# A graph layer on one core: the first four quads of the round gathered from the input rows during setup, and the weights loaded as six arrays

## The reference

```
h  = relu(layernorm(x))                       # 6250 x 128: 32 scalars, 32 vectors of 3
s  = h[:, :32] @ W_up_s / sqrt(32);  v = (h[:, 32:] as u x 3) through W_up_v / sqrt(32)
tpw = silu(silu(ef @ A1 + b1) @ A2 + b2) @ A3 # per edge, 4 x 32 weights w0..w3
message of an edge: s[src], v[src] times edge_attr and w0..w3   # 256 values
agg = segment_sum(message, dst) / 10
out = x + (agg through W_out_s, W_out_v) / sqrt(64)
```

## Time and profile before

| | us |
|---|---|
| median of 3 runs | 1932.57 (1929.12 to 1933.47) |
| the profiled execution, its own time | 1928.3 |
| its span | 1926.5 |

### The profile page before, as it was taken

The page is one execution under the profiler, slowest core; times in us unless marked ns, Lnnn a source line. Parts: engine busy times, 40 slices in busy tenths (PEclk is TensorE's granted clock), DMA queues, the critical chain, the costliest instruction groups (busy, mean ns, idle before and its releaser), DMA issues. The chain is left out here.

```text
span 1926.5 us, 69847 instructions
## 1 busy us (share of the span) xinstructions
PE 1632.5 (85%) x22862; PEld 1289.1 (67%) x22862; DVE 1340.1 (70%) x2623; ACT 403.3 (21%) x640; POOL 1424.7 (74%) x1558
## 2 busy tenths in 40 slices
PE   5898879888898898798988987988889879888895
PEld 3677667667676676676766766767667657666673
DVE  5767767676677676776776866767768667676684
ACT  4222212221122121221211211212212212222221
POOL 4777777777777777777777777777777777777774
PEclk9898889898898898998988988989889889898897
DMA  8222222222222222222222222222222222222223
GB/s 244 63 67 63 69 68 62 65 70 61 66 64 69 67 64 63 71 60 68 63 68 67 63 65 70 61 66 67 66 67 63 66 69 62 65 68 63 67 63 107
DMA packets 127196, 136.87 MB, mean 71 GB/s; under 512 B 74779, under 2 KB 96852, under 8 KB 126678
## 3 DMA queue, kind: packets, MB, share of 16 engines
q0 software_dynamic: 48096, 97.92, 20.2%
q1 hardware_dynamic: 78134, 33.75, 7.0%
q10 hardware_dynamic: 576, 0.05, 0.0%
HBM read 125.14 MB, written 6.43 MB: 68 GB/s over the span
## 5 line engine op out<-in xcount | busy, mean ns | idle before, releaser
L626 POOL DMA_INDIRECT rows<-node_table,src_in x1491 | 1407.7, 944 | 464.4 <-issue 457.3
L909 PE MATMUL pss<-tab_sb,x_sb 128*128 128x128 f32 x4704 | 635.1, 292 | 0.0
L909 PEld LDWEIGHTS pss<-tab_sb,x_sb 128*128 128x128 f32 x4704 | 598.5, 206 | 13.4 <-issue 0.2
L876 PEld LDWEIGHTS psw<-a_bd,h 64*128 64x128 f32 x3136 | 230.2, 201 | 355.6 <-DVE msgs L775 171.7
L876 PE MATMUL psw<-a_bd,h 64*128 64x128 f32 x3136 | 316.0, 318 | 146.8 <-DVE msgs L775 136.0
L773 DVE TENSOR_TENSOR msgs<-rows,psw 128x256 f32<-128x256 f32 x392 | 165.2, 421 | 363.5 <-PE psw L876 182.1
L775 DVE TENSOR_TENSOR msgs<-rows,psw 128x768 f32<-128x768 f32 x392 | 371.3, 947 | 0.0
L748 DVE TENSOR_TENSOR x_sb<-picks_in,psx 128x1024 f32<-128x1024 int32 (+1 forms) x294 | 363.1, 1236 | 0.0
L897 PE MATMUL pss<-msgs,onehot 128*32 128x64 f32 (+1 forms) x12544 | 325.0, 249 | 0.0
L669 ACT ACTIVATE sums<-pss 128x384 f32<-128x384 f32 (+1 forms) x196 | 90.7, 463 | 1037.2 <-PE pss L909 805.7
L897 PEld LDWEIGHTS pss<-msgs,onehot 128*32 128x32 f32 x12544 | 256.0, 117 | 53.6 <-issue 10.1
(11 more groups left out here) (67 smaller groups left out, 312.8 us busy)
## 6 DMA issues: line engine op xcount, KB each, us to landing
rows<-node_table SPq DMA_DIRECT2D x3072, 0.5 KB
rows<-node_table,src_in POOLq DMA_INDIRECT x1491
ef_in<-in_efT SPq DMA_DIRECT2D x100, 96.0 KB
picks_in<-in_picks SPq DMA_DIRECT2D x50, 64.0 KB
attr_in<-in_attr SPq DMA_DIRECT2D x100, 32.0 KB
xT_sb<-in_xT SPq DMA_DIRECT2D x7, 448.0 KB, 8.2
x_sb<-in_x SPq DMA_DIRECT2D x7, 448.0 KB, 8.0
out_T<-xT_sb SPq DMA_DIRECT2D x1, 3136.0 KB, 8.9
```

The costliest lines, as they stand in the source:

```text
L626: pool.indirect_dma_start(out=rows[:, quad_slot(p) + t, :], out_offset=None, in_=table, in_offset=bass.IndirectOffsetOnAxis(ap=src_in[:, b ...
L876: last = nc.tensor.matmul(edge_w[:, t * F:(t + 1) * F], h2[hid, b % HBUF, g, at:at + P], a3_bd[hid, F * r:F * (r + 1)], start=True, stop=True)
L909: last = nc.tensor.matmul(pss[:, o % 2, CH:CH + F], pick[:, t, :], tab_sb[:, t, :], start=False, stop=(r % 2 == 1 and t == PICK_BLOCKS[r + ...
```

## The change

1. POOL gathers the rows of the first four quads (16 tiles) of the round in setup, from the input `x`, which the host now lays out in the table's order of features. They go to a buffer of their own, `first_rows`, `RAW_BETWEEN` many in front of each variance.
2. In two batches of eight tiles DVE takes their statistics (`raw_statistics`, after the table rows of chunks 3 and 5), ACT the root and the ReLU with the mean subtracted (`raw_relu`, after the rows of chunk 5 and after those of chunk 6), TensorE transposes (`raw_turn`), ACT and DVE copy a half each (`raw_copy`), TensorE projects (`raw_up`), and DVE scales into `first_rows` (`raw_scale`). This goes through `ps_mlp`, `psw` and a free part of `msgs`.
3. In the round, POOL starts with quad 4, `messages` reads `first_rows` for quads 0 to 3 of iteration 0 without waiting for gathers, and POOL and SP have iteration 0 written out ahead of their loops.
4. The host lays the block-diagonal weights out; ACT loads six arrays. POOL's memsets and both engines' 24 small loads go. The scaling of `w_out` moves from POOL to DVE.
5. The three loads of the groups' values move from SP, in front of its last eight table stores, to POOL, behind the last variance.

```diff
+RAW_QUADS = 4
+RAW_BATCHES = RAW_QUADS // 2
+RB = 2 * QT
+RAW_BETWEEN = (3, 3, 3, 2, 2, 2, 1)
...
+def gathered_count(j, p, tiles):
+    return j * 16 * quad_gathers(p) + 16 * (tiles - (QT if p < RAW_QUADS else 0))
...
-                    if c == 2:
-                        sp.wait_ge(groups_stored, 32)
-                        sp.dma_start(span_row[:, :], spans_dram).then_inc(groups_back, 16)
-                        sp.dma_start(start_row[:, :], starts_dram).then_inc(groups_back, 16)
-                        sp.dma_start(start_all[:, :], starts_dram.broadcast_to([P, NW])).then_inc(groups_back, 16)
...
+                pool.wait_ge(src_first, 16 * BODY)
                 for c in range(NCH):
+                    for t in range(sum(RAW_BETWEEN[:c]), sum(RAW_BETWEEN[:c + 1])):
+                        gather_raw(t)
                     variance(c)
-                    if c == 1:
-                        load_mlp_matrices(1)
...
+                pool.wait_ge(groups_stored, 32)
+                pool.dma_start(span_row[:, :], spans_dram).then_inc(groups_back, 16)
+                pool.dma_start(start_row[:, :], starts_dram).then_inc(groups_back, 16)
+                pool.dma_start(start_all[:, :], starts_dram.broadcast_to([P, NW])).then_inc(groups_back, 16)
...
+                act.dma_start(w_up[:, :], W_up).then_inc(up_loaded, 16)
+                act.dma_start(a1_bd[:, :], A1).then_inc(mlp_loaded, 16)
+                act.dma_start(a2_bd[:, :], A2).then_inc(mlp_loaded, 16)
+                act.dma_start(a3_bd[:, :], A3).then_inc(mlp_loaded, 16)
+                act.dma_start(biases_sb[:, :], biases).then_inc(mlp_loaded, 16)
+                act.dma_start(w_out[:, :, :], W_out).then_inc(out_loaded, 16)
...
+                def raw_relu(k):
+                    n = slice(k * RB, (k + 1) * RB)
+                    act.wait_ge(raw_stats, k + 1)
+                    act.activation(raw_std[:, n], raw_var[:, n], ACT.Sqrt, scale=MUL / F,
+                                   bias=scaled_eps[:, 0:1]).then_inc(raw_std_done, 1)
+                    for t in range(k * RB, (k + 1) * RB):
+                        last = act.activation(first_rows[:, t, :], first_rows[:, t, :], ACT.Relu, bias=raw_mean[:, t:t + 1])
+                    last.then_inc(raw_relu_done, 1)
...
                 for c in range(NCH):
                     if c + 1 < NCH:
                         relu(c + 1)
                     table_rows(c)
+                    if c == NCH - 2:
+                        raw_relu(0)
+                for k in range(RAW_BATCHES):
+                    if k + 1 < RAW_BATCHES:
+                        raw_relu(k + 1)
+                    raw_copy(k)
...
+                    if c in (NCH - 4, NCH - 2):
+                        raw_statistics((c - NCH + 4) // 2)
                 place_iota()
...
+                for k in range(RAW_BATCHES):
+                    raw_copy(k)
+                    if k + 2 < RAW_BATCHES:
+                        raw_statistics(k + 2)
+                    if k >= 1:
+                        raw_scale(k - 1)
                 count_rounds()
+                raw_scale(RAW_BATCHES - 1)
...
+                raw_turn(0)
+                for k in range(RAW_BATCHES):
+                    if k + 1 < RAW_BATCHES:
+                        raw_turn(k + 1)
+                    raw_up(k)
...
-                    with sp.Fori(0, NJ - 1) as j:
+                    def iteration(j, first=False):
...
+                    iteration(0, first=True)
+                    with sp.Fori(1, NJ - 1) as j:
+                        iteration(j)
...
-                    with pool.Fori(0, NJ - 1) as j:
+                    for p in range(RAW_QUADS, QB):
+                        gather(0, p, quad_gathers(p))
+
+                    with pool.Fori(1, NJ - 1) as j:
...
+                        held = first_rows[:, QT * p:QT * p + QT, :] if first else rows[:, quad_slot(p):quad_slot(p) + QT, :]
```

210 lines of the change are left out of this document (135 added, 75 removed).

## The result

The changed kernel takes **1976.66 us** (median of four runs, 1969.86 to 1982.14) against 1931.05 of the kernel before (four runs, 1929.12 to 1933.47): a ratio of 1.0233, 95% interval 1.0215 to 1.0251. That is 45.6 us more; the prediction said 12.1 more, 1944.7, in a range up to 1954. The direction was right, the size was not.

The account below looks back on a forecast made before the run. SP's DMA issue, 76.68 us per cycle, was taken as the bound. Setup +16.1, SP's first iteration -3.7 and tail -0.3 gave +12.1 on 1928.3, so 1940.4; with medians 4.3 higher, 1944.7 us, range 1931 to 1954.

Parts of the forecast that it names:

- SP paces the round, and 16 gathers less are hidden: Round: SP's issue sets the 76.68 us cycle, so the 20.0 us POOL saves in gathers are worth nothing.
- Setup +16.1: Setup, up to SP's first load of the round: the raw work delays it from 41.42 to 57.5 us.
- SP's straight entry and slow issue, -3.7: SP's written-out first iteration: one loop turn less, -2.7 us, and perhaps no slow ef load; bounds 0 to -5.5.
- Tail, -0.3: Last half iteration and output store: nearly unchanged, as one gather wait of 0.50 us was left; 0 to -2.
- Scatter of SP +-3: SP's issues over the whole run: an allowance of 3 us either way, three slow issues like the ef load's.
- what would show it: Signs in the profile: SP's first load at 54 to 62, cycle 76.4 to 76.9, longer single waits, POOL held.
- Rival 3: SP's written-out iteration: each of its 128 singles 0.1 us slower, +13 us, 1957.7; chance 0.05.
- Rival 4: SP's issues in the round: slow ones vanish with POOL out of step, -6 us, 1938.7; chance 0.07.
- Rivals 1 and 2: Round: POOL is the bound, 1927.2, chance 0.12. Setup: the raw work hides there, 1935.6, chance 0.10.
- rival 1: Round: POOL's gathers are the bound and their 20 us saving shows, -5.4 us, 1927.2; chance 0.12.

Follow-up runs that it names:

- e: The changed kernel with the next iteration's ef, attr and dst loads issued by ScalarE instead of SP; 1930.32 us.
- p: n with the next iteration's ef, attr and dst loads issued by ScalarE instead of SP; 1926.83 us.
- o: n with 39 unread small matmuls added at the head of TensorE's setup; 1934.44 us.
- k: The kernel before with 25 unread small matmuls added at the head of TensorE's setup; 1937.28 us.
- l: The changed kernel with 39 unread small matmuls added at the head of TensorE's setup; 1959.20 us.
- n: The changed kernel with the raw gathers counted on the round's semaphores, so VectorE's loop waits for the old counts, one register instruction shorter; 1941.65 us.
- q: n with one always-met wait more in VectorE's loop, before the messages of quad 0; 1965.56 us.
- a: The kernel before without POOL's 12 gathers for quads 0 to 2 of the first iteration, whose messages read unrelated table rows; 1925.17 us.

## Why the prediction was right and wrong, step by step

- *SP paces the round, and 16 gathers less are hidden.* Right. The waits for singles grew, those for gathers went, POOL was held; e shows that what is gained off SP is gained.
- *Setup +16.1.* Right: +17.1. The last variance ended at 36.78 (36.0). Timeline after the change, PE's second turn and first projection, and DVE's last scale, to be read against the earlier trace rows:

```profile
44.77 1.94 PE L601 MATMUL ps_mlp<-identity,first_rows 128*128 128x128 f32 x8 [2.91 <-ACT msgs L426]
46.50 3.11 PE L612 MATMUL psw<-w_up,msgs 128*128 128x128 f32 x16
...
55.83 1.29 DVE L522 TENSOR_TENSOR first_rows<-psw,raw_rstd 128x512 f32<-128x512 f32 x2 [2.17 <-PE psw L612]
```

  From the start of that turn to the end of the projection are 4.84 us (4.8 predicted, between full and half clock; the granted clock was 0.61 between 45 and 50). The end was 57.1 instead of 55.7: 0.8 of that is the later variance, 0.9 the second projection, which took 3.61 and not 2.7, at a granted clock of 0.53 from 52.2 to 55.8.
- *SP's straight entry and slow issue, -3.7.* Right in kind, too small in size: the cycle with the turn removed was 4.7 shorter, and that of iteration 0 another 2.6, of which 1.1 is the slow ef load. The entry gave what was predicted (2.65 instead of 5.40 us from the last load to the next single, 139.86 - 137.21). What the sum lacked is that the written-out loads also follow each other faster: from the list's load to the end of the last dst load 4.6 us instead of 5.7. -7.3 in all, beyond my bound of -5.5.
- *Tail, -0.3.* Right: -0.2.
- ***Scatter of SP +-3.* This step failed.** The profile before had shown the effect: nine slow issues in its 22 cycles, and the 1.44 us of the earlier trace rows in iteration 0. I took them for chance that could come three times more or less, at 3 us in the whole run. They are meetings with instruction fetches, at much the same places in every cycle, and so come in most cycles or in hardly any: the stalls went from 0.27 to 2.03 us in a cycle, and 22 cycles took 40.8 us more. The prediction's "what would show it" had the cycle at 76.4 to 76.9; it was 78.50. The prediction had the sentence "three slow issues like the ef load's" where it should have asked what stood beside that load, and what in the change would move it. The change moved it twice, by longer code on TensorE ahead of its loop and by one more value in VectorE's.
- *Rival 3* put a price of 13 us on new code being slow, on the engine that was rewritten (SP), and gave it 0.05. SP's new code was not slow (its first 64 singles took 29.05 us); the code that mattered was that of two other engines, whose loops do the same work as before. *Rival 4* looked at the right step, SP's slow issues, and had the sign wrong. *Rivals 1 and 2* did not happen; p is rival 1, after SP is relieved.
- Without the stalls, o's 1934.4 lies below the 1944.7 predicted in spite of 5 us more in the setup than in the kernel after. Its 22 cycles took 9 us less than before; 4 of these are the 0.27 us of stalls that the kernel before had itself, the rest was not looked into.

## What to carry to other kernels

When one engine's DMA issues set the pace, its spare time is nil, and what disturbs single issues counts in every iteration: look at the slowest of them in the profile before, and find out what passes there. An edit that adds instructions ahead of a loop, or one in it, can move or add instruction fetches, so compare the packets of the instruction queues in both profiles before explaining a small loss by the edit's own work. The sturdy cure is not padding but to take work from the pacing engine: with 12 issues moved to ScalarE, the layout no longer mattered for SP's stalls (0.05 us with a long turn, 0.01 without).

## What the runs showed of the hardware that was not expected

- An instruction fetch (16 KB on q8 or 8 KB on q14) that passes while SP issues the load of a block can make that issue up to 1.9 us longer: after the change all 50 issues of over 0.6 us met one, and 82 others met one without stalling. The singles, 0.45 us each, met them too and took the same time in all kernels (64 in 28.6 to 29.1 us).
- TensorE's loop takes 9 or 10 fetches of 16 KB in an iteration (217 or 240 in all) for the same work, by what stands ahead of it: 25 small matmuls turn 10 into 9 in k, and with the raw chain's own, 39 turn 9 into 10 in l.
- One instruction more in VectorE's loop made its turn 3.3 us longer and took 109 fetches of 8 KB more in the run (127 to 236, n and q); with less code ahead of the loop, in a, one more did neither.
- TensorE's granted clock from 45 to 50 us was 0.61: after idle times of 3.3 and 2.9 us around a piece of 1.1, the first 3.9 us of this stretch ran at 1.2 GHz and the rest at 2.4. For the second projection, behind 2.6 idle us, it was 0.53, nearly all at 1.2 GHz. A price between the two was right for the first projection (4.84 us with the turn) and still too low for the second (3.61).
